# A two-layer decoder on one core: softplus step size made by GpSimd, an earlier placing of the last group but one, and two expert weights ahead of the rows

## The chip, the cores and the metric

The kernel runs on one core of one Trainium2 chip. The core has five engines with instruction streams of their own: TensorE (PE; its weight loads are listed as PEld), VectorE (DVE), ScalarE (ACT), GpSimd (POOL) and SyncE (SP), which mostly issues DMAs. A line of the profile that ends in q (ACTq, SPq) is an engine's instruction queue, where DMAs are issued and registers loaded. The metric is the device time of one execution in microseconds (us), as the median of several runs; lower is better.

## The reference

The input x is 64 sequences of 64 tokens with 128 features, so 4096 tokens. Two layers follow, each of three steps with a residual and a LayerNorm in front:

```
x = x + mamba(layernorm(x))                       # M:  selective scan, 256 channels, 16 states
x = x + cross_attention(layernorm(x), ctx)        # X0: 16 heads of 8, 64 keys of 96 features
x = x + experts_top2(layernorm(x))                # F0: 8 experts, 128 -> 512 -> 128, gelu
x = x + self_attention(layernorm(x))              # S1
x = x + cross_attention(layernorm(x), ctx)        # X1
x = x + experts_top2(layernorm(x))                # F1: 8 experts, gated, 128 -> 256 -> 128, silu
```

The parts that the change touches are the scan and the dispatch to experts. In the scan,

```
dt = softplus(low @ W_dt.T + b_dt)
h[t] = exp(dt[t] * A) * h[t-1] + dt[t] * B[t] * xs[t]
y[t] = sum over 16 states of h[t] * C[t]  + xs * D
```

and in the experts every token goes to the two experts with the largest of eight logits, its two answers being added with weights.

## The kernel before, in words

All tensors are fp32. Tokens are handled in 8 groups of 512 (GROUPS, GROUP), four tiles of 128 rows each.

**The scan (`mamba_phase`).** Channels lie on the 128 partitions in two halves, 512 tokens side by side. For each group c and each of 16 states n, thus for k = 16c + n from 0 to 127: ScalarE makes the decays exp(dt*A) in PSUM (`decay`, L609, one for each half), GpSimd makes u*B (`times_b`, L347, tile M_dbx, 1024 elements a partition), VectorE scans both halves (`scan`, L449), and TensorE turns the state; one half of the tokens is multiplied with C on ScalarE (L619) and summed in PSUM, the other on VectorE (`times_c`, L466). The order within each engine is written out by hand by the value of n. GpSimd may be ahead of the scan by at most the ring of four M_dbx buffers.

Meanwhile the next group's dt is prepared. softplus is log(1 + exp(-|v|)) + max(v, 0), with a correction for the rounding of the 1 +: ScalarE makes the exponential and the logarithm, VectorE the rounding (`rounding_of_1p`, after step 8, L433, which writes M_e), GpSimd subtracts the correction (`soft_fix`, after step 13, L326, M_lnv), VectorE adds the positive part (`make_dt`, after step 12, L441, M_dt; it waits for that subtraction), and GpSimd multiplies with xs (`make_u`, after step 15, L331, M_u). `times_b` of step 12 waits until the rounding is done (L345). Two halves of the residual path (L474, L481, L488) are VectorE's as well.

**Attention and dispatch (`cross_expert_phase`, X0 with F0 and X1 with F1).** Steps i of four in each group (PER) run through the attention of group c; the steps from 32 on are the tail, with no attention left in them but the last group's. The dispatch follows some steps behind. For each group VectorE adds the attention output (`residual`, L1581; X0 has a predicated copy behind it, L1585) and makes LayerNorm moments (`stats`, up to L2173), GpSimd the power -1/2 (`pool_normal`, L2125), VectorE the normalised rows (`vector_normal`, L2135), TensorE the logits, VectorE chooses two experts (`choose`, L2180 to L2204), TensorE counts ranks (`ranks`, L2291 to L2294), and VectorE makes positions of them (`place`, L2214 to L2218, tile F_pos). GpSimd then sends each group's rows to their slots in DRAM with eight indirect DMAs (`pool_scatter`, L2156), two in each step. Behind the last group's positions VectorE makes the table of blocks and `tail`; ScalarE's queue then writes a padding block behind each expert's rows (`scalar_pads`, eight DMAs, each with a register load, L2094 and L2095).

**The experts (`expert_stage`).** 39 blocks of 256 rows. `sync_blocks` on SP's queue loads the weights of a block (L2375) and its rows (L2385). There are five weight buffers and eight row buffers. As soon as the table is there it issues the weights of blocks 0 to 4, then reads three row numbers (L2380), waits in `rows_written` (L2103) for all scatters and all paddings, and issues the rows of blocks 0 to 7. TensorE turns the rows (L2513), multiplies (L2525, L2537), and GpSimd writes the answers to DRAM (L2422).

## Time and profile before

| quantity | value |
| --- | --- |
| median of 3 runs | 1583.67 us (1583.32 to 1584.39) |
| profiled execution, its own time | 1580.65 us |
| its span, first to last instruction | 1578.8 us |
| busy: PE, DVE, ACT, POOL | 1227.9, 1017.5, 905.0, 754.3 us |
| scan phase | about 0 to 460 us |
| X0 and F0 | about 460 to 950 us |
| S1 | about 950 to 1130 us |
| X1 and F1 | about 1130 to 1579 us |

The profile comes from one execution. The page gives busy time by engine, then forty slices of the span with a busy digit in each (9 means 90% or more); a slice is 39.5 us. A row of the timeline is the start in us, the duration, the engine, the source line, operation, output and inputs, the number of instructions merged in it, and in brackets the idle time before it and what ended that.

### The profile page before, as it was taken

What the parts mean: (1) busy time and instruction counts of PE and PEld (TensorE: products, weight loads), DVE (VectorE), ACT (ScalarE), POOL (GpSimd) and SP (SyncE); (2) the same over time, 40 slices, a digit from 0 to 9 for tenths busy, and PEclk for the clock granted to TensorE, in tenths of its full rate; (3) what the DMA queues carried; (4) which work ended last, traced back from release to release, by engine and by line L of the source; (5) the groups of instructions that cost most, each with busy time, mean ns of one, the idle gap of its engine ahead of it and who ended that gap; (6) DMA issues with size and microseconds to landing.
All of it is one profiled execution on the core that took longest, in us unless ns stands there. A gap on an engine that the chain in (4) does not pass through costs nothing. (4 is left out here: it accounts for less than half of the span.)

```text
span 1578.8 us, 31345 instructions
## 1 busy us (share of the span) xinstructions
PE 1227.9 (78%) x11210; PEld 942.8 (60%) x11218; DVE 1017.5 (64%) x2383; ACT 905.0 (57%) x1718; POOL 754.3 (48%) x583
## 2 busy tenths in 40 slices
PE   6898989898768887765399947998698885528882
PEld 3666766676654665544299944666456663428771
DVE  5999999999997586655111117886379665423334
ACT  3988898889745775552255526776366453213333
POOL 2998899888844133444355541110113244335552
PEclk8999999999988788776599978999799777659996
DMA  5241222132000310111579734000200011146665
GB/s 188 82 140 55 109 82 83 55 109 82 28 1 17 45 39 29 39 42 54 160 235 263 228 83 82 16 15 16 74 2 24 24 32 34 31 140 201 197 199 175
DMA packets 98028, 138.51 MB, mean 88 GB/s; under 512 B 13965, under 2 KB 77402, under 8 KB 93684
## 3 DMA queue, kind: packets, MB, share of 16 engines
q1 hardware_dynamic: 85764, 117.08, 25.1%
q0 software_dynamic: 9088, 17.07, 3.2%
q10 hardware_dynamic: 3024, 2.36, 0.5%
q8 instruction: 91, 1.49, 0.4%
q14 instruction: 61, 0.50, 0.1%
HBM read 105.91 MB, written 28.19 MB: 85 GB/s over the span
## 5 line engine op out<-in xcount | busy, mean ns | idle before, releaser
L347 POOL TENSOR_TENSOR M_dbx<-M_u,M_b_sb 128x1024 f32<-128x1024 f32 x127 | 297.2, 2363 | 41.2 <-DVE M_e L433 16.4
L449 DVE TENSOR_TENSOR_SCAN M_h<-M_pA,M_dbx 128x512 f32<-128x512 f32 x256 | 297.7, 1203 | 3.4 <-ACT M_pA L609 3.1
L609 ACT ACTIVATE M_pA<-M_dt,M_a_neg 128x504 f32<-128x504 f32 x256 | 174.9, 684 | 33.4 <-DVE M_h L449 28.4
L2525 PE MATMUL X_bank<-F_xT,F_wbuf 128*128 128x256 f32 x624 | 151.2, 386 | 0.0
L1861 PE MATMUL X_bank<-L_ident,X_s_sb 128*128 128x128 f32 x512 | 96.9, 317 | 68.0 <-ACT X_pt_sb L1724 65.1
L2156 POOL DMA_INDIRECT F_slots<-F_line,F_pos x128 | 126.7, 990 | 43.0 <-issue 39.4
L1724 ACT ACTIVATE X_pt_sb<-X_bank 128x512 f32<-128x512 f32 x128 | 76.3, 596 | 112.3 <-PE X_bank L1861 112.3
L1549 DVE TENSOR_REDUCE X_smax<-X_bank 128x8 f32<-128x512 f32 x128 | 82.2, 683 | 89.0 <-PE X_bank L1852 87.2
L619 ACT ACTIVATE M_hc<-M_pT,M_cT 128x256 f32<-128x256 f32 x256 | 119.4, 467 | 33.3 <-PE M_pT L756 31.3
L772 PE MATMUL M_pY<-M_ident,M_hc 128*128 128x128 f32 x1024 | 136.7, 277 | 0.6 <-issue 0.2
L772 PEld LDWEIGHTS M_pY<-M_ident,M_hc 128*128 128x128 f32 x1024 | 126.6, 194 | 0.4
L2125 POOL TENSOR_TENSOR F_ln_rstd<-F_ln_var_eps,F_ln_minus_half 128x4 f32<-128x4 f32 x16 | 16.6, 1039 | 225.1 <-DVE F_ln_var_eps L2173 225.1
L2525 PEld LDWEIGHTS X_bank<-F_xT,F_wbuf 128*128 128x128 f32 x624 | 114.6, 194 | 13.4 <-ACT F_xT L2485 0.5
L2485 ACT ACTIVATE F_xT<-X_bank 128x256 f32<-128x256 f32 x78 | 29.9, 383 | 158.6 <-PE X_bank L2513 133.6
L1861 PEld LDWEIGHTS X_bank<-L_ident,X_s_sb 128*128 128x128 f32 x512 | 63.5, 159 | 95.0 <-issue 92.0
L2422 POOL DMA_INDIRECT F_answers<-X_pt_sb,X_s_sb x78 | 75.7, 971 | 90.9 <-DVE X_pt_sb L2443 74.4
L756 PE MATMUL M_pT<-M_ident,M_h 128*128 128x128 f32 x512 | 80.8, 281 | 44.4 <-ACT M_hc L619 27.6
L2443 DVE TENSOR_TENSOR X_pt_sb<-X_bank,F_wbuf 128x256 f32<-128x256 f32 x39 | 16.5, 424 | 152.1 <-PE X_bank L2537 148.8
L756 PEld LDWEIGHTS M_pT<-M_ident,M_h 128*128 128x128 f32 x512 | 56.9, 141 | 96.3 <-DVE M_h L449 60.9
L2422 POOL DMA_INDIRECT F_answers<-F_yblk,F_xblk x78 | 75.8, 971 | 80.3 <-DVE F_yblk L2443 60.6
L466 DVE SCALAR_TENSOR_TENSOR M_acc<-M_pT,M_cT,M_acc 128x256 f32<-128x256 f32 x240 | 101.8, 464 | 0.8 <-PE M_pT L745 0.8
L2435 DVE SCALAR_TENSOR_TENSOR F_hT<-X_bank,F_wbuf,F_sg 128x256 f32<-128x256 f32 x78 | 34.1, 479 | 101.1 <-PE X_bank L2525 36.1
(338 smaller groups left out, 2811.0 us busy)
## 6 DMA issues: line engine op xcount, KB each, us to landing
M_b_sb<-M_rows_bc SPq DMA_DIRECT2D x32, 1024.0 KB, 4.8
F_wbuf<-in_F_wcat SPq DMA_DIRECT2D x39, 578.0 KB
F_wbuf<-in_F_wcat SPq DMA_DIRECT2D x39, 450.0 KB
X_s_sb<-F_slots SPq DMA_DIRECT2D x39, 132.0 KB
F_xblk<-F_slots SPq DMA_DIRECT2D x39, 132.0 KB
F_line<-F_line SPq DMA_DIRECT2D x16, 256.0 KB
S_ya<-F_answers SPq DMA_DIRECT2D x16, 256.0 KB, 6.1
F_slots<-F_pad ACTq DMA_DIRECT2D x16, 132.0 KB
```

The source lines that it names most:

```text
L347: pool.tensor_tensor(dbx[:, k % DBXS, :, :], u[:, g % 2, :, :], bc(b_sb[:, n, :], 1, 2), ALU.mult).then_inc(dbx_ready, 1)
L449: v.tensor_tensor_scan(h[:, k % STATES, half, :], pA[:, (2 * k + half) % DECAYS, :, :].rearrange("p b t -> p (b t)"), dbx[:, k % DBXS, hal ...
L466: ins = v.scalar_tensor_tensor(acc[:, g % 2, t, :], pT[:, 1, t, :], c_col, acc[:, g % 2, t, :], ALU.mult, ALU.add)
L609: act.activation(pA[:, (2 * k + half) % DECAYS, :, 1:SEQ], dt[:, g % 2, half, :].rearrange("p (b t) -> p b t", t=SEQ)[:, :, 1:SEQ], ACT.Ex ...
L619: act.activation(hc[:, k % SCALED, t, :], pT[:, 0, t, :], ACT.Identity, scale=cT[:, g % 2, t, n:n + 1]).then_inc(hc_ready, 1)
L756: ins = pe.transpose(pT[:, 0, t, half * P:(half + 1) * P], h[:, k % STATES, half, t * P:(t + 1) * P], ident[:, :])
L772: ins = pe.matmul(pY[:, half, t * P:(t + 1) * P], hc[:, k % SCALED, t, half * P:(half + 1) * P], ident[:, :], start=False, stop=(n == N - ...
L1549: v.tensor_reduce(smax[:, n % 4, :], pS[:, n % 4, :].rearrange("p (h k) -> p h k", k=SEQ), AX.X, ALU.max).then_inc(max_done, 1)
L1861: ins = pe.transpose(pPT[:, k * P:(k + 1) * P], s_sb[:, n % SLOTS, k * P:(k + 1) * P], ident[:, :])
L2156: pool.indirect_dma_start(slots, bass.IndirectOffsetOnAxis(pos[:, g, k, t:t + 1], 0), line[:, g % RING, k, t, :], None, bounds_check=E * C ...
L2422: pool.indirect_dma_start(answers, bass.IndirectOffsetOnAxis(xblk[:, j % XBUFS, s, D:D + 1].bitcast(I32), 0), yblk[:, j % XBUFS, s, :], No ...
L2525: ins = pe.matmul(bank[:, H0 + 2 * (j % 2) + b, c % 2 * BLOCK:(c % 2 + 1) * BLOCK], wbuf[:, j % WBUFS, c * P:(c + 1) * P], xT[:, j % 2, :] ...
```

## The change

Three edits.

1. `make_dt` moves from VectorE (after step 12) to GpSimd (after step 13, right behind `soft_fix`). The first group's stays on VectorE as `first_dt`. The sum is the same 128x1024 addition.
2. In the tail of both dispatch phases, `place` of group 6 (GROUPS - 2) moves on VectorE from behind the last group's `residual` and `stats` to ahead of them, and GpSimd issues group 6's first two scatters ahead of the last group's `pool_normal` (power and ids) and not behind.
3. `sync_blocks` loads two blocks' weights ahead of the wait for the rows, where it loaded five, and the other three between the rows: weights j, then rows j, for j = 2, 3, 4.

```diff
+            def make_dt(g):
+                reach(pool, da_ready, 2 * (g - 1) * N)
+                pool.wait_ge(fix_ready, g + 1)
+                pool.wait_ge(relu_ready, 2 * g + 2)
+                pool.tensor_tensor(dt[:, g % 2, :, :], lnv[:, :, :], relu[:, :, :], ALU.add).then_inc(dt_ready, 1)
...
                 if n == 13 and c + 1 < GROUPS:
                     soft_fix(c + 1)
+                    make_dt(c + 1)
...
-            def make_dt(g):
-                reach(v, da_ready, 2 * (g - 1) * N)
-                reach(v, u_ready, g - 1)
-                v.wait_ge(fix_ready, g + 1)
-                v.wait_ge(relu_ready, 2 * g + 2)
-                v.tensor_tensor(dt[:, g % 2, :, :], lnv[:, :, :], relu[:, :, :], ALU.add).then_inc(dt_ready, 1)
+            def first_dt():
+                v.wait_ge(fix_ready, 1)
+                v.wait_ge(relu_ready, 2)
+                v.tensor_tensor(dt[:, 0, :, :], lnv[:, :, :], relu[:, :, :], ALU.add).then_inc(dt_ready, 1)
...
-                    if n == 12:
-                        make_dt(c + 1)
...
+    EARLY_WEIGHTS = 2
...
-        for j in range(WBUFS):
+        for j in range(EARLY_WEIGHTS):
             weights(j)
-        ahead = [first_row(j) for j in range(3)]
+        ahead = [first_row(j) for j in range(EARLY_WEIGHTS)]
         d.rows_written(sp)
         for j in range(XBUFS):
-            block_rows(j, ahead[j] if j < 3 else first_row(j))
+            if EARLY_WEIGHTS <= j < WBUFS:
+                weights(j)
+            block_rows(j, ahead[j] if j < EARLY_WEIGHTS else first_row(j))
...
-                    if in_range(c - 2):
+                    if in_range(c - 2) and c - 2 != GROUPS - 1:
                         d.pool_normal(pool, c - 2)
...
                 if 14 <= i < STEPS and in_range(g):
                     d.pool_scatter(pool, g, n)
+                if g == GROUPS - 2 and n == 0:
+                    d.pool_normal(pool, GROUPS - 1)
...
+                if i == (GROUPS + 1) * PER:
+                    d.place(v, link, GROUPS - 2)
...
-                    if in_range(c - 3):
+                    if in_range(c - 3) and c - 3 != GROUPS - 2:
                         d.place(v, link, c - 3)
```

The order on GpSimd in the scan, in a middle group, before (line numbers are of the kernel before):

```order
L347 TENSOR_TENSOR M_dbx<-M_u,M_b_sb 128x1024 x5
L326 TENSOR_TENSOR M_lnv<-M_lnv,M_e 128x1024
L347 TENSOR_TENSOR M_dbx<-M_u,M_b_sb 128x1024 x2
L331 TENSOR_TENSOR M_u<-M_dt,M_xs 128x1024
L347 TENSOR_TENSOR M_dbx<-M_u,M_b_sb 128x1024 x6
```

and of the changed kernel, whose lines are numbered anew (L353 is `times_b`, L332 `make_dt`, L337 `make_u`):

```order
L353 TENSOR_TENSOR M_dbx<-M_u,M_b_sb 128x1024 x5
L326 TENSOR_TENSOR M_lnv<-M_lnv,M_e 128x1024
L332 TENSOR_TENSOR M_dt<-M_lnv,M_relu 128x1024
L353 TENSOR_TENSOR M_dbx<-M_u,M_b_sb 128x1024 x2
L337 TENSOR_TENSOR M_u<-M_dt,M_xs 128x1024
L353 TENSOR_TENSOR M_dbx<-M_u,M_b_sb 128x1024 x6
```

The addition now stands between `soft_fix` and the products of steps 14 and 15. On VectorE the row between the residual and the next scan is gone.

The order on VectorE in the tail of X0 and F0, before: the last group's residual, its moments, then group 6's places, then the last group's normalised rows.

```order
L2204 TENSOR_TENSOR F_carry<-F_carry,F_tile_sum 128x8
L1581 TENSOR_TENSOR L_x<-X_bank,L_x 128x512
L1585 COPY_PREDICATED L_x<-X_nan_mask,X_alt 128x512
L109 BN_STATS F_stats<-L_x 128x6 x4
...
L2173 TENSOR_TENSOR F_ln_var_eps<-F_ln_m,F_ln_dm 128x4
L2214 TENSOR_TENSOR F_r_3<-X_bank,F_region 128x32
L2216 TENSOR_TENSOR F_at<-F_oh,F_r_3 128x64
L2217 TENSOR_REDUCE F_at_sum<-F_at 128x8
L2218 TENSOR_SCALAR F_pos<-F_at_sum 128x8
L2135 TENSOR_SCALAR F_line<-L_x,F_ln_mean,F_ln_rstd 128x128 x4
```

and of the changed kernel:

```order
L2207 TENSOR_TENSOR F_carry<-F_carry,F_tile_sum 128x8
L2217 TENSOR_TENSOR F_r_3<-X_bank,F_region 128x32
L2219 TENSOR_TENSOR F_at<-F_oh,F_r_3 128x64
L2220 TENSOR_REDUCE F_at_sum<-F_at 128x8
L2221 TENSOR_SCALAR F_pos<-F_at_sum 128x8
L1584 TENSOR_TENSOR L_x<-X_bank,L_x 128x512
L1588 COPY_PREDICATED L_x<-X_nan_mask,X_alt 128x512
L109 BN_STATS F_stats<-L_x 128x6 x4
...
L2176 TENSOR_TENSOR F_ln_var_eps<-F_ln_m,F_ln_dm 128x4
L2138 TENSOR_SCALAR F_line<-L_x,F_ln_mean,F_ln_rstd 128x128 x4
```

The four instructions of `place` now stand ahead of the residual. GpSimd's last rows of that phase (F_ln_rstd is the power, F_slots the scatters), before:

```order
L2156 DMA F_slots<-F_line,F_pos 35072x132 x4
L2125 TENSOR_TENSOR F_ln_rstd<-F_ln_var_eps,F_ln_minus_half 128x4
L2128 COPY F_line<-F_ids 128x8
L2156 DMA F_slots<-F_line,F_pos 35072x132 x8
L2125 TENSOR_TENSOR F_ln_rstd<-F_ln_var_eps,F_ln_minus_half 128x4
L2128 COPY F_line<-F_ids 128x8
L2156 DMA F_slots<-F_line,F_pos 35072x132 x16
```

and of the changed kernel, where ten scatters, not eight, stand between the last two powers:

```order
L2159 DMA F_slots<-F_line,F_pos 35072x132 x4
L2128 TENSOR_TENSOR F_ln_rstd<-F_ln_var_eps,F_ln_minus_half 128x4
L2131 COPY F_line<-F_ids 128x8
L2159 DMA F_slots<-F_line,F_pos 35072x132 x10
L2128 TENSOR_TENSOR F_ln_rstd<-F_ln_var_eps,F_ln_minus_half 128x4
L2131 COPY F_line<-F_ids 128x8
L2159 DMA F_slots<-F_line,F_pos 35072x132 x14
```

Of the last sixteen scatters of the tail two have moved ahead of the last group's power.

On SP's queue, behind the table: before, rows of F0's start (each ISA row is a register step; the table's loads are TENSOR_LOAD):

```order
L2375 DMA F_wbuf<-in_F_wcat 128x1156
L2380 TENSOR_LOAD F_table
L2380 ISA x2
L2380 TENSOR_LOAD F_table
L2380 ISA x2
L2380 TENSOR_LOAD F_table
L2380 ISA x2
L2385 ISA
L2385 DMA X_s_sb<-F_slots 128x2x132
L2385 ISA
L2385 DMA X_s_sb<-F_slots 128x2x132
```

and of the changed kernel, from its second weights on (L2380 are the weights there, L2390 the rows):

```order
L2380 DMA F_wbuf<-in_F_wcat 128x1156
L2385 TENSOR_LOAD F_table
L2385 ISA x2
L2385 TENSOR_LOAD F_table
L2385 ISA x2
L2390 ISA
L2390 DMA X_s_sb<-F_slots 128x2x132
L2390 ISA
L2390 DMA X_s_sb<-F_slots 128x2x132
L2377 TENSOR_LOAD F_table
L2377 ISA x2
L2380 ISA
```

Before, the weights shown are the fifth; now they are the second, and the third follow behind two blocks of rows.

## Rows read from the trace of the kernel before

**Rows 1.** Page, part 2: VectorE's busy tenths in forty slices of the span.

```profile
DVE  5999999999997586655111117886379665423334
```

**Rows 2.** Windows, one scan group: us, busy PE PEld DVE ACT POOL, clock, DMA share, GB/s.

```profile
249.88:302.81 52.93, 47.38 (x318) 36.38 (x318) 52.72 (x73) 45.69 (x83) 47.42 (x24) 1.00 0.22 82
```

**Rows 3.** Timeline of VectorE, 291.7 to 297 us, around `make_dt`.

```profile
292.63 1.21 DVE L441 TENSOR_TENSOR M_dt<-M_lnv,M_relu 128x1024 f32<-128x1024 f32 x1
293.77 2.33 DVE L449 TENSOR_TENSOR_SCAN M_h<-M_pA,M_dbx 128x512 f32<-128x512 f32 x2
```

**Rows 4.** Waits in the same group: waiter, releaser, us in total, times, longest.

```profile
POOL M_dbx L347 <- DVE M_h L449: 1.0, 2, 0.7
```

**Rows 5.** Timeline of GpSimd, 277 to 310 us.

```profile
280.24 4.68 POOL L347 TENSOR_TENSOR M_dbx<-M_u,M_b_sb 128x1024 f32<-128x1024 f32 x2 [2.33 <-DVE M_e L433]
284.87 2.37 POOL L326 TENSOR_TENSOR M_lnv<-M_lnv,M_e 128x1024 f32<-128x1024 f32 x1
287.19 4.70 POOL L347 TENSOR_TENSOR M_dbx<-M_u,M_b_sb 128x1024 f32<-128x1024 f32 x2
293.93 2.35 POOL L331 TENSOR_TENSOR M_u<-M_dt,M_xs 128x1024 f32<-128x1024 f32 x1 [2.04 <-DVE M_dt L441]
```

**Rows 6.** Timeline of VectorE, the rounding at step 8 and the next group's start.

```profile
278.85 1.21 DVE L433 SCALAR_TENSOR_TENSOR M_e<-M_e1p,M_e 128x1024 f32<-128x1024 f32 x1
...
302.81 2.32 DVE L449 TENSOR_TENSOR_SCAN M_h<-M_pA,M_dbx 128x512 f32<-128x512 f32 x2
```

**Rows 7.** Timeline of the tail of X1 and F1, 1355 to 1425 us.

```profile
1373.99 0.22 PE L2294 MATMUL X_bank<-F_both,F_ones_bf 128*128 128x24 bf16 x3
1374.23 0.69 DVE L1581 TENSOR_TENSOR X_x<-X_bank,X_x 128x512 f32<-128x512 f32 x1 [1.21 <-PE X_bank L1896]
...
1376.63 0.18 DVE L2214 TENSOR_TENSOR F_r<-X_bank,F_region 128x32 f32<-128x32 f32 x1
1376.80 1.04 POOL L2125 TENSOR_TENSOR F_ln_rstd<-F_ln_var_eps,F_ln_minus_half 128x4 f32<-128x4 f32 x1 [4.22 <-DVE F_ln_var_eps L2173]
...
1377.36 0.17 DVE L2218 TENSOR_SCALAR F_pos<-F_at_sum 128x8 int32<-128x8 f32 x1
1378.75 1.18 POOL L2156 DMA_INDIRECT F_slots<-F_line,F_pos  x1 [0.64 <-issue]
...
1387.61 0.17 DVE L2218 TENSOR_SCALAR F_pos<-F_at_sum 128x8 int32<-128x8 f32 x1
...
1398.16 0.97 POOL L2156 DMA_INDIRECT F_slots<-F_line,F_pos  x1 [0.30 <-issue]
```

**Rows 8.** Timeline of the tail of X0 and F0, 722 to 792 us.

```profile
738.17 0.69 DVE L1581 TENSOR_TENSOR L_x<-X_bank,L_x 128x512 f32<-128x512 f32 x1 [3.90 <-remote]
738.89 0.73 DVE L1585 COPY_PREDICATED L_x<-X_nan_mask,X_alt 128x512 f32<-128x512 int32 x1
...
741.50 1.05 POOL L2125 TENSOR_TENSOR F_ln_rstd<-F_ln_var_eps,F_ln_minus_half 128x4 f32<-128x4 f32 x1 [4.22 <-DVE F_ln_var_eps L2173]
...
753.21 16.61 ACTq L2095 DMA_DIRECT2D F_slots<-F_pad  x8
...
775.68 7.15 SPq L2385 DMA_DIRECT2D X_s_sb<-F_slots  x8
```

**Rows 9.** Timeline of X1 and F1 again: the paddings.

```profile
1388.54 16.77 ACTq L2095 DMA_DIRECT2D F_slots<-F_pad  x8
```

**Rows 10.** The chain that ended last, 1360 to 1460 us: start, us, what.

```profile
1392.28 1.39 ACTq L2094
...
1401.55 0.34 ACTq L2095
...
1404.97 4.87 DMA F_slots<-F_pad
...
1410.00 2.26 DMA F_xblk<-F_slots
...
1420.41 1.73 PE X_bank L2525 x8
```

More of the change, by code:

```diff
@@ L412, in first_products @@
                 v.tensor_tensor(lnv[:, :, :], lnv[:, :, :], e1[:, :, :], ALU.subtract).then_inc(fix_ready, 1)
-                make_dt(0)
+                first_dt()
                 v.wait_ge(dt_ready, 1)
```

## The prediction, made blind

> **What bounds the kernel now.** I read the page's slices first: VectorE is at nine tenths or more through slices 2 to 10, which is the scan phase [rows 1]. Then one steady scan group by windows: in 52.93 us VectorE is busy 52.72, TensorE 47.38, ScalarE 45.69 and GpSimd 47.42 [rows 2]. The reader is to see that only VectorE has no room; GpSimd has 5.5 us of it. The timeline around `make_dt` says what one of its instructions costs there, the waits and GpSimd's timeline how much of GpSimd's room is waiting for VectorE [rows 3 to 5]. The tails of the two dispatch phases I read by their timeline and the chain of waits, for what releases the first block of rows [rows 7 to 10].
>
> **Edit 1, `make_dt`.** It goes from VectorE in 7 of 8 groups. It starts at 292.63 and the next scan at 293.77 [rows 3], so it costs 1.14 us of VectorE's stream (its 1.21 overlaps its neighbour a little). 7 x 1.14 = 8.0 us, if VectorE stays the bound. Next in line are TensorE and ScalarE, which would have 4.4 and 6.1 us left in a group of 51.8.
>
> GpSimd takes it on. Its own row for such an addition is the correction, 284.87 to 287.19 when the next begins: 2.32 us [rows 5]. From 280.24, the product of step 12, the new row of work is: two products to 284.87, the correction to 287.19, dt to 289.51, two products (as now, 287.19 to 291.9, thus 4.65) to 294.16, u (2.35) to 296.5, next group's first product (2.32) to 298.8. The wait of 2.04 for VectorE's dt [rows 5] is gone, and u now ends at 293.93 + 2.35 = 296.28, so GpSimd gets there 0.2 to 0.3 us later than now. VectorE wants that product at 302.81 now [rows 6] and at 301.67 then: 2.8 us to spare. So the scan doesn't wait. ScalarE's decays of the next group want dt at about the same 302; it comes at 289.5 in place of 293.8, so nothing is late there.
>
> Over a whole group GpSimd's 47.42 becomes 49.74, in a period of 51.79. It now waits 2.33 for the rounding [rows 5], 2.04 for dt and 1.0 for free buffers [rows 4], 5.4 in all, and needs 2.32 + 1.14 = 3.46 of it. Fits, with 2 us over.
>
> What comes close is the rounding, L433. VectorE runs it at 278.85, and GpSimd is idle from 280.24 - 2.33 = 277.91, so the product of step 11 ends 0.94 before it [rows 5, 6]. GpSimd will be later against VectorE by 0.28 + 1.14 = 1.42, of which the buffer waits of 1.0 [rows 4] take up to 1.0. The product then ends between 0.5 us ahead of the rounding and 0.5 us behind its start. What two such instructions do to each other no row shows: in the rows the rounding runs alone. From below it costs nothing (the scans, with one operand in PSUM, run beside products all the time and still follow one another without a gap [rows 2, 3]); from above VectorE waits for the rest of the product, 0.5 us in each of 7 groups, 3.5 us. I take nothing, the row that it is nearest to being the scan beside a product. The Trainium skill ("SBUF — State Buffer", section on the two separate sides) says that a VectorE instruction with two SBUF inputs and a GpSimd instruction that reads SBUF take a shared port pair as an exclusive lock, the later one blocking until the other is done; the rounding has two SBUF inputs. By that rule the upper end holds for each overlap, and the gain of edit 1 would be between 4.5 and 8.0. No run here shows it yet.
>
> **Edit 2, places and two scatters ahead.** In F1 the residual starts at 1374.23, released by TensorE's output projection; the rank sums that `place` needs end at 1374.21 [rows 7]. So `place` can start at about 1374.35. It is 0.73 us from the first of its four instructions to the last, and the next follows 0.08 later: the residual comes 0.93 later than now, and so do the moments. Positions are ready at 1374.35 + 0.90 = 1375.25. From the power's end, 1377.84, to the first scatter is 0.91 now; with that the two scatters run from 1376.15 for 1.18 + 0.30 + 0.97 = 2.45 [rows 7], to 1378.6. The power, at 1376.80 now, has its input at 1377.7 but must queue behind them: +1.8 us. Behind it wait the normalised rows, the logits, the choice, the table, and thus the paddings, all +1.8. `place` was hidden by the power before, so nothing is won back on VectorE.
>
> On GpSimd the 4.22 us wait ahead of the power [rows 7] is used for 2.5 us of scatters, but behind the power (to 1379.6) the first of the other six starts at 1380.5 and they end near 1388.2, at 1.27 each, while the last group's positions come at 1387.78 + 1.8 = 1389.6. So GpSimd waits, and its last scatter is at 1398.16 + 1.2 us [rows 7] rather than earlier.
>
> In F0 the same, but the residual has 0.73 us of predicated copy behind it [rows 8], so the scatters nearly fit: residual +0.93 (738.17 to 739.1), positions 739.2, scatters from 740.1 to 742.5, power at 742.5 for 741.50: +1.0; the last scatter about +0.4.
>
> By itself edit 2 costs 1.8 + 1.0 = 2.8 us if the paddings stay the last thing waited for.
>
> **Edit 3, two weights.** The first rows wait for the last padding: it is issued at 1404.97 and lands 4.87 us later, while up to five weight loads share the DMA engines; the row read issued right after, alone and of the same size (256 rows of 132 numbers), takes 2.26 [rows 10]. With two weight loads, both issued before 1401.5, the last padding should have the queues to itself: 4.87 - 2.26 = 2.6 us in F1. In F0 the last padding's issue ends at 753.21 + 16.61 = 769.82 and the rows go at 775.68, 5.86 later; in F1 it ends at 1405.31 and they go at 1410.00, 4.69 later [rows 8 to 10]. So F0 has 1.2 more to give: 3.8. From below the landing gains nothing; from above these 2.6 and 3.8, which I take.
>
> How much of edit 2's delay reaches the last padding? ScalarE's queue goes slowly, some 0.7 us for each step, from the third padding on, and is quick again at 1401.55, 2.4 us after the last scatter's end at 1399.13 [rows 7, 10]. If the scatters hold it up, the last padding moves with them (+1.2 in F1, +0.4 in F0); if not, with the table (+1.8, +1.0). I take the middle, 1.5 and 0.7. Net: F1 -1.1, F0 -3.1.
>
> Of the weights moved behind, block 2's are wanted when TensorE comes to them: its products start at 1420.41, 10.4 us after the first rows' issue [rows 10]. What stands ahead of them now is two reads of rows; even if the weights took the 4.87 of a crowded padding behind the 2.26 of a read, they are there after some 7 us. The cover is TensorE's first two blocks, so I cost it at nothing; without it, up to 4.9 a phase.
>
> **Sum.** 8.0 + 3.1 + 1.1 = 12.2 us. Against the profiled execution's 1580.65 (span 1578.8 and 1.85 around it) that is 1568.5; the median of the runs is 3.0 higher, so 1571.5 us.
>
> **The rivals.**
> - *The dispatch edits don't pay.* The landing stays as it is, because the paddings' own queue and not the weights makes it long; edit 2's delay is then passed on whole: -8.0 + 2.8 = -5.2, 1578.5 us. For it: ScalarE's queue takes 1.39 us for a register load already at 1392.28, and reads and writes of DRAM need not take the same [rows 10]. Against: the 2.26 us of the row read.
> - *The scan gives less.* The rounding meets GpSimd's product: 4.5 in place of 8.0, with the rest as forecast, 1575.0. Or TensorE, at 47.4 of 52.9, holds steps back once VectorE is quicker: the same size.
> - *GpSimd becomes the bound (slower).* If its waits for buffers and for the rounding don't shrink, as when each product must still start behind the same VectorE instruction and the rounding in turn waits for a whole product, dt comes on top of the period: 2.32 x 7 = 16.2 us added and the 8.0 given back, +8.2; with the dispatch's -4.2, +4.0: 1587.7. It decides from the point at which GpSimd reaches step 12 after VectorE's rounding, that is with more than 2.33 us lost in a group. Against it: I find 1.4 lost.
> - *Nothing to be seen.* The change does what it says on VectorE, but the phases end as now because another wait takes it up, within 3 us of 1583.7.
>
> **How the numbers follow.** Forecast 0.52, dispatch edits don't pay 0.20, the scan gives less 0.18, nothing 0.05, GpSimd the bound 0.05. A measurement of this kernel can tell about 0.2%, 3.2 us, from no change. The first three are faster by more than that: 0.90; 0.05 the same, 0.05 slower. The forecast's own range is 1569 to 1574; the range to 1578 takes in most of the two cases beside it, and 1568 allows for the last padding not being delayed at all.
>
> **What would show it.** Right: scan groups of 51.8 us by windows with VectorE still full; GpSimd's dt at 2.3 us and its wait for the rounding near 1 us; the last power 1.8 us (F1) and 1.0 us (F0) later against its residual's release; the last padding's landing near 2.3 us. Wrong: a gap ahead of the rounding or a longer rounding; scans that wait for M_dbx; a last padding that still takes 4 us or more; or TensorE waiting for the weights of blocks 2 to 4.

## The result, and the profile after

| | before | after |
| --- | --- | --- |
| median | 1584.03 us (4 runs, 1583.32 to 1585.27) | 1558.61 us (4 runs, 1554.15 to 1565.75) |
| ratio | | 0.9845, 95% interval 0.9818 to 0.9872 |
| profiled execution, span | 1580.65, 1578.8 us | 1554.15, 1552.4 us |

The change is faster by 25.4 us; 12.2 were forecast. In the two profiles the span is 26.4 us shorter. It was gained here (each row ends at an event both profiles have; "last maximum" is the attention's last L1549 of before):

| up to | before | after | gained in this stretch | forecast |
| --- | --- | --- | --- | --- |
| end of the scan | 458.34 | 453.58 | 4.8 | 8.0 |
| X0, first maximum | 501.25 | 495.37 | 1.1 | 0 |
| X0, last maximum | 711.87 | 697.39 | 8.6 | 0 |
| F0, first rows issued | 775.68 | 754.95 | 6.3 | 3.1 |
| X1, last maximum | 1348.29 | 1329.65 | -2.1 | 0 |
| F1, first rows issued | 1410.00 | 1385.54 | 5.8 | 1.1 |
| end | 1578.79 | 1552.36 | 2.0 | 0 |

One scan group of the changed kernel by windows answers [rows 2]; the columns are the same:

```profile
246.95:299.27 52.32, 46.98 (x318) 36.43 (x318) 51.60 (x71) 45.23 (x83) 49.70 (x25) 1.00 0.22 83
```

The group fell from 52.93 to 52.32, not to 51.79, and VectorE now has 0.72 us in it without work. Its timeline says where: ahead of step 2's scan.

```profile
253.75 0.87 DVE L486 SCALAR_TENSOR_TENSOR M_y_sum<-M_xs,M_d_skip,M_pM 128x256 f32<-128x256 f32 x2
255.34 2.34 DVE L454 TENSOR_TENSOR_SCAN M_h<-M_pA,M_dbx 128x512 f32<-128x512 f32 x2 [0.72 <-ACT M_pA L612]
```

GpSimd's timeline in the same group answers [rows 5]. The new row is L332, 2.33 us to the next start. The wait for dt is gone, the wait for the rounding is not shorter.

```profile
273.13 2.37 POOL L353 TENSOR_TENSOR M_dbx<-M_u,M_b_sb 128x1024 f32<-128x1024 f32 x1
277.82 4.69 POOL L353 TENSOR_TENSOR M_dbx<-M_u,M_b_sb 128x1024 f32<-128x1024 f32 x2 [2.33 <-DVE M_e L440]
282.47 2.37 POOL L326 TENSOR_TENSOR M_lnv<-M_lnv,M_e 128x1024 f32<-128x1024 f32 x1
284.97 2.37 POOL L332 TENSOR_TENSOR M_dt<-M_lnv,M_relu 128x1024 f32<-128x1024 f32 x1
287.30 4.67 POOL L353 TENSOR_TENSOR M_dbx<-M_u,M_b_sb 128x1024 f32<-128x1024 f32 x2
```

The tail of X0 and F0 answers [rows 8] (timeline). The residual starts right behind the places, two scatters run, then the power; the last eight scatters wait for their positions; the eight paddings are issued in 8.72 us where before took 16.61.

```profile
725.13 0.17 DVE L2221 TENSOR_SCALAR F_pos<-F_at_sum 128x8 int32<-128x8 f32 x1
725.21 0.69 DVE L1584 TENSOR_TENSOR L_x<-X_bank,L_x 128x512 f32<-128x512 f32 x1
...
726.10 1.38 POOL L2159 DMA_INDIRECT F_slots<-F_line,F_pos  x1 [3.23 <-DVE F_pos L2221]
...
728.78 1.06 POOL L2128 TENSOR_TENSOR F_ln_rstd<-F_ln_var_eps,F_ln_minus_half 128x4 f32<-128x4 f32 x1
...
741.24 0.97 POOL L2159 DMA_INDIRECT F_slots<-F_line,F_pos  x1 [3.14 <-DVE F_pos L2221]
...
741.40 8.72 ACTq L2098 DMA_DIRECT2D F_slots<-F_pad  x8
...
754.95 0.96 SPq L2390 DMA_DIRECT2D X_s_sb<-F_slots  x2
```

In F1 it is the same against [rows 7, 9]:

```profile
1356.73 0.69 DVE L1584 TENSOR_TENSOR X_x<-X_bank,X_x 128x512 f32<-128x512 f32 x1
...
1359.88 1.05 POOL L2128 TENSOR_TENSOR F_ln_rstd<-F_ln_var_eps,F_ln_minus_half 128x4 f32<-128x4 f32 x1
...
1372.30 8.54 ACTq L2098 DMA_DIRECT2D F_slots<-F_pad  x8
...
1385.54 0.95 SPq L2390 DMA_DIRECT2D F_xblk<-F_slots  x2
```

What the first rows wait for has changed, too. Before, it was the last padding [rows 10]. The chain that ended last in the changed kernel, at the same place in F1, goes through the last scatter; its landing takes 3.98 us:

```profile
1381.28 3.98 DMA F_slots<-F_line,F_pos
...
1385.54 2.25 DMA F_xblk<-F_slots
```

Attention gained 8.6 us in X0, though no edit touches it. The windows of the stretch between scan and X0, and of X0's attention, before and then after, show the granted clock of TensorE (third number from the end) at 0.80 and 0.79, then at 0.88 and 0.85:

```profile
458.34:501.25 42.91, 31.68 (x161) 19.65 (x162) 31.56 (x101) 14.27 (x24) 22.42 (x23) 0.80 0.03 7
501.25:711.87 210.62, 166.30 (x2043) 120.68 (x2044) 139.77 (x420) 129.12 (x233) 66.71 (x69) 0.79 0.16 39
```

```profile
453.58:495.37 41.79, 30.35 (x161) 19.00 (x162) 31.60 (x101) 14.28 (x24) 22.43 (x23) 0.88 0.03 7
495.37:697.39 202.02, 156.91 (x2043) 113.41 (x2044) 140.59 (x421) 128.80 (x233) 66.91 (x69) 0.85 0.17 40
```

So three things are open: why the scan gives 4.8, what the clock has to do with the edits, and why the dispatch gives 12.1 and not 4.2.

### The profile page after: what moved, and what is told of

It reads as the page before. It is cut to its first block and busy times, and to the rows that moved or that the text cites. A ratio compares the mean times of both kernels' runs of the same rounds, so it can differ in the third digit from the quotient of the medians.

```text
span 1552.4 us, 31341 instructions
## 1 busy us (share of the span) xinstructions
PE 1214.8 (78%) x11210; PEld 936.1 (60%) x11218; DVE 1011.3 (65%) x2376; ACT 902.7 (58%) x1718; POOL 771.3 (50%) x590
## 3 DMA queue, kind: packets, MB, share of 16 engines
q10 hardware_dynamic: 3024, 2.36, 0.5%
## 5 line engine op out<-in xcount | busy, mean ns | idle before, releaser
L353 POOL TENSOR_TENSOR M_dbx<-M_u,M_b_sb 128x1024 f32<-128x1024 f32 x127 | 296.8, 2364 | 33.2 <-DVE M_e L440 15.5
L622 ACT ACTIVATE M_hc<-M_pT,M_cT 128x256 f32<-128x256 f32 x256 | 119.8, 469 | 42.9 <-PE M_pT L759 41.5
L2532 PEld LDWEIGHTS X_bank<-F_xT,F_wbuf 128*128 128x128 f32 x624 | 115.8, 196 | 13.7 <-ACT F_xT L2492 0.4
L2128 POOL TENSOR_TENSOR F_ln_rstd<-F_ln_var_eps,F_ln_minus_half 128x4 f32<-128x4 f32 x16 | 16.7, 1042 | 209.7 <-DVE F_ln_var_eps L2176 209.6
L2450 DVE TENSOR_TENSOR X_pt_sb<-X_bank,F_wbuf 128x256 f32<-128x256 f32 x39 | 16.6, 425 | 142.7 <-PE X_bank L2544 136.1
```

The costliest lines, as they stand in the source:

```text
L353: pool.tensor_tensor(dbx[:, k % DBXS, :, :], u[:, g % 2, :, :], bc(b_sb[:, n, :], 1, 2), ALU.mult).then_inc(dbx_ready, 1)
L622: act.activation(hc[:, k % SCALED, t, :], pT[:, 0, t, :], ACT.Identity, scale=cT[:, g % 2, t, n:n + 1]).then_inc(hc_ready, 1)
L2532: ins = pe.matmul(bank[:, H0 + 2 * (j % 2) + b, c % 2 * BLOCK:(c % 2 + 1) * BLOCK], wbuf[:, j % WBUFS, c * P:(c + 1) * P], xT[:, j % 2, :] ...
```

## The experiments

They ran on several chips, which turned out to be of two kinds. On five the kernel before takes 1463 to 1468 us; on one it takes 1585, as in the result above (whether the result's chip is that one is not on record; its rows look the same). Only numbers of one kind are compared. Ratios are against the kernel before on the same chip.

**The edits one by one** (other kind of chip). e1 is edit 1, e2 edit 2, e3 edit 3, e4 edits 2 and 3; each is the part of the diff shown above.

> Edit 1 alone. Theory A (each edit acts by itself; ScalarE takes part of the scan's gain): first group 1.1 us shorter, the others 0.6 each, scan end 4.8 us earlier, nothing else: ratio 0.997 (about 1579.3 for 1584). Theory B (the rest of the gain, too, hangs on edit 1, because attention after a shorter scan gets a higher granted clock): X0's attention is 8 us shorter as well, 1571. The prediction's own figure was -8.0 in the scan.

> Edit 2 alone, all five weights still ahead of the rows. Prediction: costs 1.0 in F0 and 1.8 in F1, 1586.8. Theory C (the slow steps of ScalarE's queue, 0.7 us each, start when GpSimd has issued about nine scatters without a gap, and edit 2 puts a gap behind the eighth): the eight paddings are issued at 1.1 us each instead of 2.1, the first rows come 4 to 6 us earlier in each phase: 1574 or so. Theory D (the slow steps come from five weight loads in flight): the paddings stay slow, 1585.

> Edit 3 alone, sixteen scatters in a row as before. Prediction: -3.8 in F0 and -2.6 in F1: 1577.6, paddings' issues still slow (16.6 us for eight). Theory C: paddings slow until 2.4 us after the last scatter, then the last one lands in about 2.3: 1578. Theory D: the paddings are issued quickly (1.1 us each), rows then wait for the last scatter's landing: 1572 or so.

> Edits 2 and 3 without edit 1. Theory A: F0's first rows come 7.8 us earlier and F1's 7.0 earlier against their own last residual, as in the changed kernel; with 1.9 in the experts behind: 1567. Theory B: X0's attention is not shorter without edit 1. If that part of the changed kernel's gain comes with edits 2 and 3 or by itself, X0's attention is 8.6 us shorter here too, and the whole is 1563 or less.

Next, the changed kernel and the kernel before again, and edits 1 and 3 without 2:

> The changed kernel once more, on the chip of the experiments. Edit 1 alone was 1.24% faster there than the kernel before and edits 2 and 3 together 0.2%. Theory A (edit 1 brings its scan gain and, through a higher granted clock in the attention behind it, some 13 us more; edits 2 and 3 little on this chip): 0.986, about 1446 for 1467. Theory E (edit 1 alone was a lucky draw of the clock): 0.993 to 0.996.

> The kernel before, for its profile on this chip. Ratio 1.000. If the 0.7 us steps of ScalarE's and SyncE's queues ahead of the experts (16.6 us for eight paddings) belong to the kernel, they are here; if they belong to the chip of the first profiles (theory F), the paddings take 8 us and the groups of the attention phases have no stall of all queues of 4.2 us.

> Edits 1 and 3 without 2. If edit 2 costs what the prediction said (1.0 and 1.8 us), this is 3 us faster than the changed kernel; if its gap in the scatters is what keeps the queues quick, it is slower, by 8 us where the slow steps appear and not at all where they don't.

| kernel | ratio (95% interval) | scan end to X0 | X0 attention | last maximum to first rows, F0, F1 |
| --- | --- | --- | --- | --- |
| e6, before | 1.0004 (0.9979 to 1.0029) | 42.9 | 180.1 | 53.4, 50.0 |
| e1, edit 1 | 0.9876 (0.9832 to 0.9921) | 41.8 | 172.0 | 53.3, 49.5 |
| e2, edit 2 | 1.0027 (1.0001 to 1.0054) | 43.0 | 180.1 | 55.3, 51.4 |
| e3, edit 3 | 0.9983 (0.9962 to 1.0005) | 41.3 | 174.0 | 52.0, 50.5 |
| e4, edits 2, 3 | 0.9980 (0.9952 to 1.0007) | 42.8 | 183.2 | 53.1, 52.9 |
| e8, edits 1, 3 | 0.9891 (0.9853 to 0.9930) | 41.9 | 172.1 | 51.0, 46.7 |
| e5, all three | 0.9926 (0.9891 to 0.9962) | 41.9 | 172.1 | 53.3, 49.0 |

The last three columns are of one profile each. Three things follow. On this kind of chip the ratio of all three edits, 0.9926, is what was forecast (1571.5 / 1583.67 = 0.9923), but not by the forecast's terms: that is luck. Edit 3 brings the first rows 2.3 and 2.8 us sooner (e1 against e8), edit 2 puts them 2.3 and 2.3 us later (e8 against e5): here the two cancel, and by these rows the change is better without edit 2; the ratios can't tell, their intervals overlap. Other pairs say less: edit 3 by e6 and e3 gives 1.4 us less in F0 and 0.5 more in F1, edit 2 by e3 and e4 1.1 and 2.4 more. In F1 these are mixed with the clock, for the granted clock between the last maximum and the residual is 0.88 in e6 and 0.72 and 0.71 in e3 and e4. And in no profile of this kind, not even of before, do the paddings take 16 us: before's row here is

```profile
716.75 7.82 ACTq L2095 DMA_DIRECT2D F_slots<-F_pad  x8
```

On these chips the last scatter is what the first rows wait for in every F1 profile, before's too: its landing takes 5.4 to 6.1 us where five weights are loaded ahead of the rows (5.48 in e6) and 2.4 to 4.0 where two are (2.80 in e3, 2.36 in e8, 3.74 in e5). So edit 3 shortens a landing as forecast, but the scatter's and not the padding's.

Edit 1 by itself brings 1.24%, 18 us, in five executions. The scan gives some 4.7 of it by the lengths of its groups; X0's attention and the stretch ahead of it give 9.2 more, at the higher clock (0.88 and 0.92, e6 had 0.80 and 0.87). The remaining 4 us are not located: the profiles of e1 and e6 are only 8.8 us apart, X1's attention being 2.2 us longer in e1's. By the profile, theory B of e1's text describes what happens, though not why, as will be seen. The changed kernel itself (0.9926) lies nearer to theory E of e5's text than to its 0.986. Theory F holds: the 0.7 us steps are not the kernel's alone. C and D of e2 and e3 could not be told apart here, where there are no slow steps.

**Where the scan's gain went.** e7 is the changed kernel with:

```
                 if n == 1 and c < GROUPS:
+                    decay(k + 1, 0)
                     if c + 1 < GROUPS:
                         silu_x(c + 1)
                     silu_z(c)
...             (at n == 2: decay(k, 1) alone, ahead of both scale_c)
```

> The changed kernel with ScalarE's first decay of step 2 issued ahead of the two silu and the table loads of step 1, and the second one right behind them. Theory G (the missing 0.54 us of each scan group is the wait of VectorE at step 2 for that decay, 0.72 us): the groups go from 52.32 to about 51.85, scan end 3 us earlier, 1.0 us of the groups' period being left at TensorE or ScalarE otherwise. Theory H (TensorE or ScalarE holds the group at 52.3 whatever that order): groups stay at 52.3.

Its group by windows, and VectorE's timeline at step 2:

```profile
243.95:295.99 52.04, 46.45 (x318) 36.56 (x318) 51.81 (x71) 44.88 (x83) 49.67 (x25) 1.00 0.22 83
```

```profile
251.54 1.22 DVE L454 TENSOR_TENSOR_SCAN M_h<-M_pA,M_dbx 128x512 f32<-128x512 f32 x1
252.92 1.22 DVE L454 TENSOR_TENSOR_SCAN M_h<-M_pA,M_dbx 128x512 f32<-128x512 f32 x1 [0.16 <-ACT M_pA L612]
```

The wait of 0.72 became 0.16, and the group 52.04: theory G, with half of its gain given back, since VectorE's own instructions came to 51.81 instead of 51.60. Theory H falls. In both kernels two silu and two table loads stand between ScalarE's decays there; in the changed kernel the decay of 248.72 is followed by that of 254.62. The whole stayed at 0.9931 (0.9901 to 0.9961): the lower clock of X0 took the gain back (scan end to X0 42.7 us at 0.80, attention 179.4).

e12 asks how much room GpSimd really had:

```
+                pool.tensor_tensor(dt[...], lnv[...], relu[...], ALU.add).then_inc(again, 1)
+                pool.wait_ge(again, g)
                 pool.tensor_tensor(dt[...], lnv[...], relu[...], ALU.add).then_inc(dt_ready, 1)
```

> The changed kernel with dt made twice on GpSimd, 2.3 us more in each of seven groups. Forecast's reckoning: GpSimd has 52.3 - 49.7 = 2.6 us left, 2.33 of it waiting for the rounding, so the second dt just fits: groups 52.3 to 52.6, GpSimd's wait for the rounding gone or near it. Rival (GpSimd becomes the bound as soon as it comes late to step 12): groups of 54 us or more, +12 us in the scan.

Groups of 53.49 us: neither. VectorE's and GpSimd's timelines at step 8:

```profile
278.16 2.39 DVE L443 SCALAR_TENSOR_TENSOR M_e<-M_e1p,M_e 128x1024 f32<-128x1024 f32 x1
280.48 1.21 DVE L457 TENSOR_TENSOR_SCAN M_h<-M_pA,M_dbx 128x512 f32<-128x512 f32 x1
```

```profile
274.80 4.67 POOL L356 TENSOR_TENSOR M_dbx<-M_u,M_b_sb 128x1024 f32<-128x1024 f32 x2
280.72 4.67 POOL L356 TENSOR_TENSOR M_dbx<-M_u,M_b_sb 128x1024 f32<-128x1024 f32 x2 [1.25 <-DVE M_e L443]
```

GpSimd is late enough that its product (to 279.47) overlaps the rounding's start at 278.16, and the rounding takes 2.39 where it takes 1.22 alone: it ends 1.08 after the product's end, so it did its work behind it. It costs 1.17 in each group. In the groups of five of the eight it is 2.4 to 2.9 us, in the other three 1.22. The Trainium skill ("SBUF — State Buffer", two separate sides) calls the port pair that such two instructions need an exclusive lock, the later one blocking until the earlier one is done. The trace agrees with it. In the changed kernel the product ended at 275.50 and the rounding began at 276.44, so they did not meet, and all eight roundings took 1.21 to 1.23 us.

**Whose is the clock's gain?** e10 is the kernel before with needless work, e11 the changed kernel with the same:

```
             def skip_last(g):
                 v.wait_ge(yb_psum, g + 1)
+                for r in range(3 if g == 4 else 0):
+                    ... (the two instructions below once more)
+                    ins.then_inc(again, 1)
+                    v.wait_ge(again, r + 1)
```

> The kernel before with three needless repetitions of a pair of VectorE's instructions in one scan group: everything behind it comes 2.3 us later, no work is saved. Theory K (what X0's attention gains in the changed kernel comes from where the end of the scan falls against the clock's levels, and not from the edit itself): 2.3 us less or more there can change the 42.9 us between scan and X0 to 41.8 and X0's attention from 180 to 172, so the kernel with more work gets faster, by up to 6 us. Theory L (the shorter and fuller scan groups of edit 1 keep the clock up): attention stays at 180 and the whole is 2.3 us slower, 1.0016.

> The changed kernel with the same 2.3 us of needless work. Theory K: the granted clock between scan and X0 goes from 0.88 back to 0.80 and X0's attention from 172 to 180: +10 us. Theory L: +2.3 us, attention stays at 172.

e10's scan ends 2.5 us later than e6's, and e10 is faster than before: 0.9964 (0.9943 to 0.9985). e11 is no faster than before, 1.0004 (0.9976 to 1.0032), where the changed kernel had 0.9926. Windows of the same two stretches, for e10 and for e11:

```profile
458.63:500.37 41.74, 30.39 (x161) 19.06 (x162) 31.59 (x101) 14.29 (x24) 22.43 (x23) 0.88 0.03 7
500.37:672.38 172.01, 146.50 (x2046) 106.66 (x2046) 143.34 (x420) 128.12 (x233) 61.02 (x63) 0.92 0.19 46
```

```profile
453.16:495.74 42.58, 31.35 (x161) 19.51 (x162) 31.58 (x102) 14.27 (x24) 22.42 (x23) 0.80 0.03 7
495.74:675.63 179.89, 154.78 (x2046) 113.23 (x2046) 142.66 (x420) 128.56 (x233) 61.04 (x63) 0.87 0.18 44
```

Needless work that makes the scan 2.5 us (e10) or 1.8 us (e11) longer swaps 0.80 and 0.88 in either kernel, so theory L falls, and the 8 us are not won by the work that edit 1 takes off VectorE. Theory K holds in that the timing decides, but not the time of the scan's end itself: e11's scan ends at 453.16 and e1's at 453.45, with 0.80 and 0.88 behind them. What goes with the clock in the 18 profiles, on both kinds of chip, is how long the scan takes from its second group's start to its end:

| scan, us | profiles | clock behind it |
| --- | --- | --- |
| 361.8 | e7, e9 | 0.80 |
| 363.6 | the seven with edit 1 and no other edit of the scan | 0.88 |
| 365.4 | e11 | 0.80 |
| 367.3 | before, e2, e3, e4, e6, e13 | 0.80, e3 0.83 |
| 369.6 | e10, e12 | 0.88 |

X0's attention follows it on the result's kind of chip, too: 210.6 and 210.0 us without edit 1 (before, e13), 202.0 and 202.7 us with it (the changed kernel, e14).

In the nine profiles with 0.88 the clock stays at its full level to the scan's end and then is at 1.2 GHz (0.50) for 10.2 us in all. In the nine others it has fallen to 1.2 GHz once or twice already around the start of the last scan group, and behind the scan it is there for 17.1 us (e3 13.7). Windows of the result's kernel before: one such fall, in which TensorE is busy 3.37 of 3.40 us, and the one behind the scan.

```profile
403.50:406.90 3.40, 3.37 (x17) 3.05 (x17) 3.40 (x6) 2.24 (x5) 3.40 (x3) 0.50 0.00 0
464.90:482.00 17.10, 10.15 (x30) 7.17 (x31) 14.74 (x66) 1.19 (x2) 11.00 (x15) 0.50 0.04 7
```

So edit 1 brought the better clock each time, but by the length that it happened to give the scan: 1.8 us less or more and it was gone. Why these lengths is open.

e9 puts edits 1, 3 and the early decay together, for the best version by terms:

> Edits 1 and 3 and ScalarE's early decay, without edit 2: the scan 6.6 us shorter than before, first rows 2 us earlier in each dispatch. By these terms alone 0.993 (about 1455 for 1465). With the higher granted clock in X0 (172 us of attention) 0.988, without it (180 us) 0.993.

It got 0.9944 (0.9909 to 0.9979), with X0 at 180.0 us and 0.87: its scan is 6.5 us shorter than e6's, and it has the worse clock. The time is that of its terms without the clock.

**The slow queues.** e13 and e14 ran on the chip of the 1585 us kind. e14 is edits 1 and 3 with the part of edit 2 that is VectorE's. e13 is the kernel before with one more wait in `pool_scatter`:

```
         if n == 0:
+            if g == GROUPS - 1:
+                pool.wait_ge(table_ready, 1)
             pool.wait_ge(pos_ready, g + 1)
```

> The kernel before, with GpSimd waiting for the table of blocks between group 6's eight scatters and the last group's eight: a gap of about 3 us in a run of sixteen. Theory C (the run's length brings on the slow steps): the eight paddings are issued in 8 us as in the changed kernel, wherever before takes 16. Theory F (they belong to a chip, and this one has none of them): paddings 8 us with or without the gap, last scatter 3 us later, first rows 0 to 3 us later.

> Edits 1 and 3 and only VectorE's half of edit 2: group 6's places ahead of the last residual, its scatters still behind the last power. Against edits 1 and 3 (0.989) the last power comes 0.9 us later in each phase and not 2.4 and 1.8; with the changed kernel at 0.9926 this should be at 0.990.

The paddings in F0 by timeline, first e14 (two weights, sixteen scatters in a row), then e13 (five weights, eight, a gap of 4.42, eight):

```profile
740.63 16.90 ACTq L2098 DMA_DIRECT2D F_slots<-F_pad  x8
...
746.25 7.03 SPq L2380 DMA_DIRECT2D F_wbuf<-in_F_wcat  x2
```

```profile
746.71 0.98 POOL L2158 DMA_INDIRECT F_slots<-F_line,F_pos  x1 [0.30 <-issue]
...
748.27 8.21 ACTq L2095 DMA_DIRECT2D F_slots<-F_pad  x8
...
752.11 0.97 POOL L2158 DMA_INDIRECT F_slots<-F_line,F_pos  x1 [4.42 <-DVE F_table L2240]
```

Theory C holds in kind: sixteen in a row go with 16.6 to 16.9 us for the paddings (before, e14), a run that is split with 8.0 to 8.7 (e13, the changed kernel), in F0 and F1 alike. Theory D falls, for e14 has only two weight loads ahead. How many scatters in a row it takes was not tested, nor what in the long run slows the queues. From the last maximum to the first rows, F0 and F1: before 63.8 and 61.7, e14 61.2 and 59.9, e13 59.0 and 57.1, the changed kernel 57.6 and 55.9. A gap alone is worth 4.8 and 4.6 us, although it puts the last scatter later. Against e14 the changed kernel has only GpSimd's part of edit 2 more, the two scatters ahead of the power, and that is worth 3.6 and 4.0 us. And e14, whose first rows still wait for the last padding, shows what edit 3 does to that landing: 1.79 us in F1, where before had 4.87 [rows 10].

```profile
1394.11 1.79 DMA F_slots<-F_pad
```
e14 came to 0.9881 (0.9841 to 0.9920); e13 ran once, at 1569.5 for a median of 1585.2, and before itself went down to 1571.8 there, so for e13 the profile speaks and not the time.

The same mark is in X0's attention of the result's profiles, before and after: six scatters in a row, and from the fourth on VectorE and ScalarE start nothing for over 4 us, four times (timelines of VectorE and GpSimd, before; on the other chips L1572 follows at once):

```profile
605.39 1.29 DVE L1558 SCALAR_TENSOR_TENSOR X_s_sb<-X_bank,X_smax 128x512 f32<-128x512 f32 x2
610.13 0.36 DVE L1572 RECIPROCAL X_rden<-X_bank 128x32 f32<-128x32 f32 x1 [3.46 <-remote]
```

```profile
605.33 0.97 POOL L2156 DMA_INDIRECT F_slots<-F_line,F_pos  x1 [0.30 <-issue]
...
608.86 1.28 POOL L1540 TENSOR_TENSOR X_alt<-X_alt,L_x 128x512 f32<-128x512 f32 x1
```

X1's attention in the same profile says more on the run's length. Its last run is ten scatters, from 1329.03 to 1340.63, and beside it no other engine starts anything for 8.57 us from 1334.75 on (timeline of VectorE and the run's last scatter):

```profile
1343.32 0.36 DVE L1572 RECIPROCAL X_rden<-X_bank 128x32 f32<-128x32 f32 x1 [8.98 <-remote]
```

```profile
1340.63 0.97 POOL L2156 DMA_INDIRECT F_slots<-F_line,F_pos  x1 [0.30 <-issue]
```

e6 has the same run of ten without a stall. But X1's three runs of six do not stop the others as X0's four do (no pause above 2.9 us), so the length is not the whole condition. Nor are the stalls all that sets this chip apart: they are 16.7 of the 30.5 us by which X0's attention is longer than e6's, and 8.6 of 42.2 in X1, the granted clock being 0.79 and 0.82 there for 0.87 and 0.98.

e15 and e16, one kernel, split those six: `if s == 3 and c < GROUPS: a.pool_add_bias(pool, c)` in place of the two calls at `s == 0`. In X0 that is one step earlier, in X1 three steps later.

> The changed kernel with GpSimd's addition of the bias one step earlier, in the middle of a run of six scatters: runs of four with an addition between. Theory C (a run of more than about four scatters makes the queues stand still, where that appears): on the chip of the first profiles the four stalls of 4.2 us in X0's attention are gone, X0's attention 202 to below 185 us, the whole under 1540. On the other chips, which show no stall: no change from the changed kernel, 0.992. Rival M (the stalls come from something else at that place, SyncE's copy of the rows and store of x): stalls stay.

> The changed kernel with runs of four scatters in the attention, as before. Where the stalls appear: X0's attention 202 to below 185 us and the whole 1.5% faster than the changed kernel (theory C), or the stalls stay (rival M). Where they don't: 0.987 to 0.992 of before.

Both times it ran on a chip without the stalls, so the split is not tested for the attention, and rival M stands. It was still the best of the versions with all edits: 0.9873 (0.9827 to 0.9920) and 0.9887 (0.9839 to 0.9935), against 0.9926 for the changed kernel; the intervals overlap, and in the profile of the first X1's attention was 159.6 us at a clock of 0.99, e5's 162.0 at 0.97. e1 and e8 are as fast. That it beats the changed kernel here is not shown; what it does where the stalls are is open.

## Why the prediction was right or wrong

The direction was right, the size was not: 1571.5 forecast with a range of 1568 to 1578, 1558.6 measured.

- *Edit 1, "7 x 1.14 = 8.0 us, if VectorE stays the bound": the step that was mis-sized.* It measured 4.8. The first group gave 1.15, the next six 0.61 each. I asked what ScalarE had left over a whole group (6.1 us) and not in the stretch behind step 1, where two silu and two table loads stand between two decays; VectorE waited 0.2 there before already, and 0.7 now. The rival "the scan gives less" had the size nearly (4.5), but named the rounding and TensorE. e7 shows that it is in good part ScalarE's order: with one decay ahead of the silu the wait is down to 0.16.
- *GpSimd.* dt took 2.33 (2.32 forecast). Its wait for the rounding was forecast near 1 us and stayed 2.33. Of the delay of 1.42 half a microsecond never came, the group being 0.61 shorter and not 1.14, and the waits for buffers, 1.0 before [rows 4] and none in the same group after, took the rest. The rounding and the product kept their 0.94 us of distance. My bounds for their meeting were right in kind: e12 measures 1.17 for an overlap of 1.31.
- *Edit 2's delay.* Against the attention's last maximum the power came 1.7 us later in F1 (1.8 forecast) and 1.8 in F0 (1.0), where the residual itself came 1.5 later.
- *"ScalarE's queue goes slowly, some 0.7 us for each step" and "If the scatters hold it up, the last padding moves with them (+1.2 in F1, +0.4 in F0); if not, with the table": the step that failed.* The two scatters put first and the waits behind them split a run of sixteen into two, six and eight, and the slow steps went away. I took them for a property of the place that the edit would shift, and never asked what makes them. Forecast for the dispatch -4.2; measured -12.1 up to the first rows of both. The scatters put first, which I counted as a cost, gave 3.6 and 4.0 of it (e14 against the changed kernel). The condition of the sum, "if the paddings stay the last thing waited for", broke with it: the rows now wait for the last scatter. On chips without slow steps the edit costs what was forecast and a little more (2.3 and 2.3 us up to the first rows, where 1.0 and 1.8 were forecast).
- *Edit 3.* The mechanism was right: e14's last padding in F1 lands in 1.79 us for 4.87, 3.1 us less where 2.6 was forecast. The sign "the last padding's landing near 2.3 us" can't be read in the changed kernel, where it is the scatter's 3.98 us that count. On the other chips the edit gives 2.3 (F0) and 2.8 (F1) by e1 against e8, forecast 3.8 and 2.6. The weights moved behind cost nothing seen: TensorE waits for no weights in the 25 us behind the first rows.
- *Not in the forecast at all:* 8.6 us in X0 and 1.1 ahead of it, from a clock that changes with the scan's length. No term and no rival had it. The scan alone would have given 1574.7; the dispatch's 7.9 more or the clock's 9.7 takes that below the range's 1568, either one by itself. X1's attention gave 2.0 back (204.9 to 206.9 us), at 0.82 in both, and F1's experts gained 2.0; the causes are open.
- *A reading.* The nines of [rows 1] run to slice 12, not 10, which is where the scan ends. No term hangs on it.

The rivals: "dispatch edits don't pay" is wrong on the result's chip and nearly right on the others, where edits 2 and 3 together measure 0.9980 (0.9952 to 1.0007). "GpSimd the bound" needs a second dt, and then costs 1.2 us a group and not 2.3, as the price is what the rounding loses behind the product.

## What to carry to other kernels

An engine with room over a period can still be the next bound in one step of it: before counting on a gain of the full engine, find its shortest wait in the period and what stands ahead of the engine that ends it. When a queue is slow in one stretch, ask what is running beside it all that time before assuming that it stays slow; here a gap in that neighbour's work was worth more than the work moved. When an edit shortens the last wait of several, look which one ends last afterwards. And where the granted clock of a stretch changes with a few microseconds of work ahead of it, a kernel with less work can be slower and the reverse: put a small needless delay in as a control before you credit an edit.

## What was not expected of the hardware

- On one chip of six, long runs of indirect DMAs on GpSimd go with slow instruction queues of the other engines: eight DMA issues of ScalarE take 16.6 to 16.9 us beside sixteen in a row and 8.0 to 8.7 us where the run is split. In X0's attention no other engine begins anything for 4.2 us in four runs of six, and in X1's for 8.6 us in a run of ten, while three runs of six there do nothing of the kind. On the five others nothing like it is seen with the same order. What makes the difference between the chips is open; it goes with 1585 us for 1465.
- The granted clock of the stretch behind the scan is 0.80 or 0.88 by 1.8 to 2.5 us more or less of scan, and not in one direction: 0.80, 0.88, 0.80, 0.80, 0.88 from the shortest scan to the longest. X0's attention takes 180 or 172 us with it. Before, TensorE is at its full level (2.4 GHz) for nearly the whole scan, falls to 1.2 GHz twice, shortly, around the start of the last scan group (at 403.5 and 417.2 us), being busy nearly all that time, and is at 1.2 GHz for 17.1 us behind the scan, of which it is busy 10.2.
- Twelve executions of the changed kernel on one chip lay from 1443 to 1464 us with mean clocks from 0.927 down to 0.911, the longer ones at the lower clock; before's twelve lay from 1460 to 1471 at 0.917 to 0.906. The better clock is not had every time, and a profile is one execution.
- A VectorE instruction with two SBUF inputs that begins 1.3 us before the end of GpSimd's product ends 1.08 us after it and takes 2.39 us, where alone it takes 1.22 (e12).
- On the five chips the last indirect DMA of F1's dispatch takes 5.4 to 6.1 us to land with five weight loads issued ahead of it, and 2.4 to 4.0 with two.
